# A graph layer's front: small TensorE products beside the edge products, W's parts moved to GpSimd, and row statistics split in two halves

## The reference, cut to what matters

```python
h = jnp.maximum(_layernorm(x, axis=-1), 0.0)
# first layer: attention over the edges
h = h @ W + b_w
s_dst, s_src = h @ a[:512], h @ a[512:]
e = leaky_relu(s_dst[dst] + s_src[src] + b_a, 0.2)
w = exp(e)
out = segment_sum((w / segment_sum(w, dst)[dst])[:, None] * h[src], dst)
x = x + out
# second layer: the same normalisation, 4 experts of two neighbour-mean
# convolutions each, the best two by a gate mixed
```

## Time and profile before

| | us |
|---|---|
| median of 3 runs | 744.05 (743.88 to 745.36) |
| the profiled execution | 744.08 |
| its span in the trace | 742.3 |
| PE busy | 717.8 (97%) |
| DVE busy | 428.0 (58%) |
| ACT busy | 398.1 (54%) |
| POOL busy | 184.1 (25%) |

### The profile page before, as it was taken

The page is one execution under the profiler, slowest core; times in us unless marked ns, Lnnn a source line. Parts: engine busy times, 40 slices in busy tenths (PEclk is TensorE's granted clock), DMA queues, the critical chain, the costliest instruction groups (busy, mean ns, idle before and its releaser), DMA issues.

```text
span 742.3 us, 12047 instructions
## 1 busy us (share of the span) xinstructions
PE 717.8 (97%) x3574; PEld 582.2 (78%) x3574; DVE 428.0 (58%) x1056; ACT 398.1 (54%) x897; POOL 184.1 (25%) x204
## 2 busy tenths in 40 slices
PE   5899999999999999999999999999999999999994
PEld 3589977888888888777777777878888888888883
DVE  8899889999752538622722622657444544444341
ACT  6966769677653521511511511347677667767751
POOL 4000000000000100850300010045666555655511
PEclk9999999999999999999999999999999999999998
DMA  9100000111501247799699695379844994438950
GB/s 207 39 4 3 4 3 18 53 35 35 165 8 58 79 123 240 217 333 326 228 354 328 200 359 197 99 184 264 300 93 88 264 343 120 86 69 225 290 156 6
DMA packets 46444, 115.19 MB, mean 155 GB/s; under 512 B 8340, under 2 KB 8552, under 8 KB 46361
## 3 DMA queue, kind: packets, MB, share of 16 engines
q1 hardware_dynamic: 28581, 77.60, 32.7%
q0 software_dynamic: 9136, 19.65, 11.6%
q10 hardware_dynamic: 8644, 16.86, 6.9%
HBM read 64.89 MB, written 50.08 MB: 155 GB/s over the span
## 4 chain that ended last, share of the span: by engine, by line
PE 92%; DVE 4%; ACT 1%; issue 1%; POOL 0%; DVEq 0%; ACTq 0%; POOLq 0%
PE ps L1783 16%; PE ps L1784 16%; PE ps L1785 16%; PE ps L2185 7%; PE ps L2184 6%; PE ps L2052 3%; PE ps L2053 3%; PE ps L1985 3%; PE ps L1860 3%; PE ps L1979 3%; PE ps L1980 3%; PE ps L2115 2%; PE ps L1923 1%; PE ps L1811 1%; PE ps L1925 1%; PE ps L1924 1%
## 5 line engine op out<-in xcount | busy, mean ns | idle before, releaser
L1110 ACT ACTIVATE agn<-ps,rec 32x128 f32<-32x128 f32 x336 | 120.7, 359 | 38.7 <-PE ps L2185 34.8
L1044 ACT ACTIVATE slots<-he_t 125x512 fp32r<-125x512 f32 x40 | 25.3, 635 | 150.9 <-DVE he_t L1581 146.6
L2185 PE MATMUL ps<-slots,CTs 125*128 x230 | 89.9, 391 | 0.0
L1581 DVE TENSOR_TENSOR he_t<-ps,b_b 125x512 f32<-125x512 f32 x40 | 27.6, 691 | 105.5 <-PE ps L1785 72.3
L728 POOL DMA_INDIRECT hrow<-t_d,piece_i x80 | 76.1, 951 | 25.7 <-issue 23.5
L2184 PE MATMUL ps<-slots,CTs 125*128 x207 | 80.7, 390 | 0.0
L1746 DVE TENSOR_TENSOR tm<-ps,b_b 128x512 f32<-128x512 f32 x23 | 15.9, 692 | 84.3 <-PE ps L1785 84.2
L1783 PE MATMUL ps<-W,agT_hi 128*125 128x512 f32 x160 | 63.5, 397 | 0.0
L1783 PE MATMUL ps<-W,h2T_hi 128*125 128x512 f32 x160 | 63.4, 396 | 0.0
L1785 PE MATMUL ps<-W,agT_lo 128*125 128x512 f32 x160 | 63.3, 396 | 0.0
L1784 PE MATMUL ps<-W,agT_hi 128*125 128x512 f32 x160 | 63.2, 395 | 0.0
(11 more groups left out here) (316 smaller groups left out, 1665.4 us busy)
## 6 DMA issues: line engine op xcount, KB each, us to landing
he_d<-slots SPq DMA_DIRECT2D x30, 448.0 KB
slots<-he_d SPq DMA_DIRECT2D x30, 448.0 KB
w_d<-slots SPq DMA_DIRECT2D x3, 4096.0 KB, 18.7
slots<-w_d SPq DMA_DIRECT2D x24, 512.0 KB
t_d<-he_t SPq DMA_DIRECT2D x40, 224.0 KB
raw<-in_L_gnn_Wl ACTq DMA_DIRECT2D x4, 1024.0 KB, 7.2
raw<-in_L_gnn_Wr ACTq DMA_DIRECT2D x4, 1024.0 KB, 5.6
slots<-in_L_gnn_Wl ACTq DMA_DIRECT2D x4, 1024.0 KB, 10.0
```

The costliest lines, as they stand in the source:

```text
L1110: last = a.activation(agn[32 * r:32 * r + 32, q, :], ps[n, 3 + i % 2, 128 * r:128 * r + 128], ACT.Copy, scale=rec[n, i, 4:5])
L2185: last = mm(o, CTs[:, t, :], part(k, P, t * 1024 + D, P), start=False, stop=t == T - 1)
```

## The change

- **Small products on TensorE.** `wake()` runs 12 products of `ones` and `ident` (128x128, f32) ahead of the first hot block. `keep_busy(bank, n)` runs n products of 250 columns of `onehot_p` whose result is never read: 3 ahead of each hot block from block 11 on, 16 behind the last block, 8 ahead of the first and 4 ahead of each other count step of tile 1. `e_q` and `q_sel` have 128 rows instead of 65; the added rows of `q_sel` are zero.
- **Order of the front.** The small steps of PE stand one or two blocks later. All 22 hot blocks are evicted by ACT. The columns of tile 0 come after block 13 instead of 10, `bias_in(0)` after 17 and `norm(0)` after 18.
- **W's parts by GpSimd.** `W0_hi` (was ACT's) and `W0_lo` (was DVE's) are made by POOL as soon as W is in SBUF, after `a_sum`, the sum of the two vectors a, with which the bias needs one product instead of two.
- **Row statistics in two halves.** Tiles 0 to 4 before tile 0's one-hots, with their own root on ACT and `scales(0)` after the first step of one-hots; tiles 5 to 9 in rounds 1 to 3 of DVE, their root behind `windows_out(3)`, `scales(1)` in round 4.
- **Round 0.** The source vectors are made four before and four after `hT_lo`. PE runs the product with W first, by parts as they come, and then the scores, which wait for `wa` alone; the bias sum is made in round 5 and waited for in the last round.

```diff
@@ -140,18 +140,19 @@
...
         e_g = at("e_g", [CR, CG, P], F32, 12032)
-        e_q = at("e_q", [2 * CR + 1, CG, P], F32R, 15040)
+        e_q = at("e_q", [128, CG, P], F32R, 15040)
...
         q_f = at("q_f", [2 * CR + 1, P], F32, 21408)
-        q_row = at("q_row", [2 * CR + 1, P], F32, 21920)
-        q_at = at("q_at", [2 * CR + 1, CR], F32, 22432)
-        q_sel = at("q_sel", [2 * CR + 1, CR, P], F32R, R1 + 20480)
+        q_row = at("q_row", [128, P], F32, 21920)
+        q_at = at("q_at", [128, CR], F32, 22432)
+        q_sel = at("q_sel", [128, CR, P], F32R, R1 + 20480)
...
         spill = [at(f"spill_{k}", [128, D], F32, R1 + 6144 + 2048 * k) for k in range(2)]
+        a_sum = at("a_sum", [P, D], F32, R1 + 18432)
@@ -618,7 +617,7 @@
...
                                      base=-CR * k, pattern=[[-1, CR]], channel_multiplier=1))
-            link(g.memset(q_at[2 * CR:, :], 1.0))
+            link(g.memset(q_at[2 * CR:2 * CR + 1, :], 1.0))
@@ -646,6 +645,13 @@
...
+            pool.wait_ge(*small_in(48))
+            g.tensor_tensor(a_sum[:], a_b[0:P, 0, :], a_b[0:P, 1, :], ALU.add).then_inc(ab_ready.sem, 1)
+            pool.wait_ge(*w0_in(16))
+            g.tensor_copy(W0_hi[:], W0_f[:]).then_inc(w0_hi_ready.sem, 1)
+            pool.wait_ge(*w0_hi_ready(1))
+            g.tensor_tensor(W0_lo[:], W0_f[:], f32(W0_hi[:]), ALU.subtract).then_inc(w0_lo_ready.sem, 1)
@@ -805,7 +811,13 @@
...
+            def deviations(k):
+                half = slice(k * T // 2, (k + 1) * T // 2)
+                a.activation(std[:, half], std[:, half], ACT.Sqrt).then_inc(std_ready.sem, 1)
...
             def norm(t):
+                if t == T // 2:
+                    act.wait_ge(*norm_ready(2))
@@ -813,12 +825,16 @@
...
                 act.wait_ge(*hw_done(t + 1))
+                if t == 0:
+                    act.wait_ge(*wa_ready(1))
...
                     act.wait_ge(*hw_done(b))
+                if b == 1:
+                    act.wait_ge(*s_done(1))
@@ -836,21 +852,21 @@
...
             for u in range(NU):
-                if u in HOT_ACT:
-                    hot_columns(u)
-                if u == 3:
+                hot_columns(u)
+                if u == 5:
...
                     copy(e_gc[:], ps[0:P, 7, 0:CG * CR]).then_inc(cols_ready.sem, 1)
-                if u == 10:
+                if u == 13:
...
                     act.wait_ge(*var_ready(1))
-                    a.activation(std[:], std[:], ACT.Sqrt).then_inc(std_ready.sem, 1)
-            act.wait_ge(*norm_ready(1))
-            norm(0)
-            act.wait_ge(*w0_in(16))
-            copy(W0_hi[:], W0_f[:]).then_inc(w0_hi_ready.sem, 1)
+                    deviations(0)
+                if u == 17:
+                    bias_in(0)
+                if u == 18:
+                    act.wait_ge(*norm_ready(1))
+                    norm(0)
@@ -865,9 +881,13 @@
...
                     a.activation(spark[:], spark[:], ACT.Exp)
-                bias_in(b)
+                if b > 0:
+                    bias_in(b)
...
                     windows_out(b)
+                if b == 3:
+                    act.wait_ge(*var_ready(2))
+                    deviations(1)
@@ -1151,14 +1171,15 @@
...
             v.memset(q_row[CR:2 * CR, :], -1.0)
+            v.memset(q_row[2 * CR:, :], 0.0)
             link(v.tensor_tensor(q_f[2 * CR:, :], q_f[2 * CR:, :], q_f[2 * CR:, :], ALU.mult))
-            link(v.tensor_scalar(q_row[2 * CR:, :], q_f[2 * CR:, :], -1.0, 1.0, ALU.mult, ALU.add))
+            link(v.tensor_scalar(q_row[2 * CR:2 * CR + 1, :], q_f[2 * CR:, :], -1.0, 1.0, ALU.mult, ALU.add))
...
                 c = slice(8 * k, 8 * k + 8)
-                v.tensor_tensor(q_sel[:, c, :], q_row[:].unsqueeze(1).broadcast_to([2 * CR + 1, 8, P]),
-                                q_at[:, c].unsqueeze(2).broadcast_to([2 * CR + 1, 8, P]), ALU.mult
+                v.tensor_tensor(q_sel[:, c, :], q_row[:].unsqueeze(1).broadcast_to([128, 8, P]),
+                                q_at[:, c].unsqueeze(2).broadcast_to([128, 8, P]), ALU.mult
@@ -1184,20 +1205,15 @@
...
-            def hot_columns(u):
-                dve.wait_ge(*hot_made(u + 1))
-                v.tensor_scalar(onehot_p[:, u * CU:(u + 1) * CU, :].rearrange("p (h c) n -> p h (c n)", h=2),
-                                ps[0:P, u % 3 * 2:u % 3 * 2 + 2, 0:CU // 2 * P], 0.0, None, ALU.max
-                                ).then_inc(hot_dve_ready.sem, 1)
+            def batch_flags(b):
+                more = more_here(dve, b)
+                return more, dve.value_load(tab_b[0:1, b:b + 1, BW + 1:BW + 2], min_val=0, max_val=NW * NG)
...
-            dve.wait_ge(*x_in(32))
-            row_stats(range(0, 2))
-            hot_columns(HOT_DVE[0])
@@ -1216,10 +1232,11 @@
...
             v.tensor_scalar(tab_f[:, 1:2], tab_f[:, 1:2], -1.0, None, ALU.add).then_inc(n_ready.sem, 1)
-            row_stats(range(2, 4))
+            dve.wait_ge(*x_in(32))
+            row_stats(range(0, 1))
...
             v.tensor_copy(tab_f[:, 2:3], ps[0:NW, 7, 0:1]).then_inc(tab_f_ready.sem, 1)
-            row_stats(range(4, T // 2))
+            row_stats(range(1, 2))
@@ -1236,38 +1253,42 @@
...
-            dve.wait_ge(*x_late_in(32))
-            link(row_stats(range(T // 2, T)))
-            for t in range(T):
-                last = v.bn_aggr(x_mv[:, t, :], x_stats[:, t, :])
-            link(last)
-            v.tensor_scalar(std[:], x_mv[:, :, 1], EPS, None, ALU.add).then_inc(var_ready.sem, 1)
+            late = row_stats(range(2, T // 2))
+            dve.wait_ge(*flag_ready(2))
+            dve.wait_ge(*tab_ready(1))
+            first_flags = batch_flags(0)
...
+            def half(k):
+                return slice(k * T // 2, (k + 1) * T // 2)
...
+            def variances(k, last):
+                link(last)
+                for t in range(T)[half(k)]:
+                    last = v.bn_aggr(x_mv[:, t, :], x_stats[:, t, :])
+                link(last)
+                v.tensor_scalar(std[:, half(k)], x_mv[:, half(k), 1], EPS, None, ALU.add).then_inc(var_ready.sem, 1)
...
+            variances(0, late)
...
-            def scales():
-                dve.wait_ge(*std_ready(1))
-                link(v.reciprocal(rstd[:], std[:]))
-                v.scalar_tensor_tensor(shift[:], x_mv[:, :, 0], -1.0, rstd[:], ALU.mult, ALU.mult
+            def scales(k):
+                dve.wait_ge(*std_ready(k + 1))
+                link(v.reciprocal(rstd[:, half(k)], std[:, half(k)]))
+                v.scalar_tensor_tensor(shift[:, half(k)], x_mv[:, half(k), 0], -1.0, rstd[:, half(k)], ALU.mult, ALU.mult
...
             def sources():
-                dve.wait_ge(*w0_in(16))
-                dve.wait_ge(*small_in(48))
-                source_vectors(0)
                 source_vectors(1)
-                for w in range(2):
-                    dve.wait_ge(*wa_f_ready(2 * KC - 1 + w))
-                    v.scalar_tensor_tensor(spill[w][0:P, :], bw_b[:], 1.0, a_b[0:P, w, :], ALU.mult, ALU.mult,
-                                           accum_out=ab[:, w:w + 1]).then_inc(ab_ready.sem, 1)
...
+            def bias_source():
+                dve.wait_ge(*ab_ready(1))
+                v.scalar_tensor_tensor(a_sum[:], bw_b[:], 1.0, a_sum[:], ALU.mult, ALU.mult,
+                                       accum_out=ab[:, 0:1]).then_inc(ab_ready.sem, 1)
                 dve.wait_ge(*ab_ready(2))
-                v.tensor_scalar(s_add[:], ab[:, 0:1], ab[:, 1:2], ba_c[:], ALU.add, ALU.add).then_inc(wa_ready.sem, 1)
...
-            def first_weights_low():
-                dve.wait_ge(*w0_hi_ready(1))
-                v.tensor_tensor(W0_lo[:], W0_f[:], f32(W0_hi[:]), ALU.subtract).then_inc(w0_lo_ready.sem, 1)
+                v.tensor_scalar(s_add[:], ab[:, 0:1], ba_c[:], None, ALU.add).then_inc(wa_ready.sem, 1)
@@ -1286,8 +1307,7 @@
...
             def tile_and_batch(b):
-                more = more_here(dve, b)
-                before = dve.value_load(tab_b[0:1, b:b + 1, BW + 1:BW + 2], min_val=0, max_val=NW * NG)
+                more, before = batch_flags(b) if b > 0 else first_flags
@@ -1301,20 +1321,35 @@
...
                     last.then_inc(step_ready.sem, 1)
+                    if b == 0 and k == 0:
+                        scales(0)
+                    if b == 4 and k == 2:
+                        scales(1)
...
                     product_low(b - 1)
-                else:
-                    scales()
-                    sources()
+                if b == 0:
+                    dve.wait_ge(*w0_in(16))
+                    dve.wait_ge(*small_in(48))
+                    source_vectors(0)
...
                 if b == 0:
-                    first_weights_low()
+                    sources()
+                if b == 1:
+                    dve.wait_ge(*x_late_in(32))
+                    row_stats(range(5, 7))
+                if b == 2:
+                    row_stats(range(7, 9))
+                if b == 3:
```

(61 more changed lines are left out.)

7 lines of the change are left out of this document (2 added, 5 removed).

## The result

The changed kernel took 746.29 us (median; 745.61 to 747.88) against 744.67 (743.88 to 745.42) for the kernel before, a ratio of 1.0029 with a 95% interval of 1.002 to 1.0037. So it is slower by 1.6 us where 2.1 us of gain were forecast. The kernel before has two groups of executions (four at 743.88 to 744.06, four at 745.29 to 745.42) and 744.67 lies between them; against 744.0, near its profiled execution (744.08) and its later medians, the loss is 2.3 us. The profiled execution of the kernel after took 745.61 us, its fastest, with a span of 743.9.

A forecast was written before the change was run, and what follows sets the result against it. The front before 42.96 us, ending in a chain on DVE alone, was taken as the bound. DVE free for tile 1 at 38.7 gives 40.75 - 38.7 = 2.05 us off 744.1: 742.0 us, range 739.8 to 745.8.

The forecast's parts named there:

- The clock and ACT's pace: Front: PE at 2.4 GHz from about 9 us, ACT's 22 blocks every 0.91 us, last done at 32.4 against 34.9.
- rival B: Front: clock not held between early blocks, ACT starves, its end 34 to 35.5; about 743.8 us; chance 0.23.
- S: Moment when DVE is free for tile 1: 37.2 us if nothing holds it, 38.7 with the collision, 42.8 before.
- The collision: Before tile 1: POOL's 3.7 us subtraction blocks DVE's first one-hots of tile 0, costing 1.65 us at the scales; chance 0.38.
- Tiles 1 to 4: On DVE: 6.15 us a tile plus 4.3 us of added work against some 2.6 of slack; gain 40.75 - S.
- The bias sum (1.0) in tile 5: DVE's later rounds: the 1.0 us bias sum and the last tile's wait for it fall into slack.
- PE's limit: Tiles 0 and 1 on PE: 6.8 us, then 6.8 plus 2.6 of small products; at most 4.1 us gained.
- (A): No collision: POOL finds gaps or one-hots don't take its port; gain 3.55, 740.5 us, at best 740.0; chance 0.27.
- (C): Slower: clock stays at 1.2 GHz into blocks with added products, each 1.5 us; 746.5 us; chance 0.12.
- (D): Small products run but move nothing, hidden by DVE's waits; up to 1 us less gain; no chance of its own.

The follow-up runs named there:

- e9: Changed kernel with flags read ahead, statistics undivided, W's low part in four pieces, and no small products (128 rows kept): 741.66 us, ratio 0.9974 to the kernel before.
- e6: Changed kernel with flags read ahead, row statistics undivided and POOL's subtraction for W's low part in four instructions of 512: 741.34 us, ratio 0.9961 to the kernel before.
- e1: Changed kernel with the next round's flags (register loads) read right behind this round's one-hots: 743.37 us, ratio 0.9990 to the kernel before.
- e10: Changed kernel with flags read ahead, statistics undivided and W loaded ahead of x's second half: 743.83 us, ratio 0.9997 to the kernel before.
- e4: Changed kernel without any small product, 128 rows kept: 746.82 us (745.7 to 751.52), ratio 1.0049 to the kernel before.
- e7: e6 without the 24 small products in tile 1: 740.81 us (739.97 to 742.36), ratio 0.9956 to the kernel before.
- e11: Kernel before with only the 128 rows and all the small products added: 747.0 us, ratio 1.0034 to the kernel before.
- e8: Kernel before with only W's high and low parts moved to POOL: 743.12 us, ratio 0.9997 to the kernel before.

## Why the prediction was wrong, step by step

*The clock and ACT's pace: right in its result.* ACT's first hot block starts at 9.80 (forecast 9.75), the last is done at 32.3 (32.4), tile 0 turns at 32.36. The clock did fall at 14 us (rival B's condition), but B's price was not due: ACT waited 0.54 us once. That this was the small products' work is not borne out: e9, without them, is only 1.4 us later at tile 0 (33.62, against 32.21 in e6 and 35.93 before), and how the other 2.3 divide between the 128 rows and the order no run shows.

*S, the moment when DVE is free for tile 1: right without the loads.* Forecast 38.7 with the collision; `wa` ended at 38.06, and the one-hots started at 39.70. The 1.64 us between are the step that failed, here for the first of three times: "DVE is free for tile 1" was taken as the moment when its last instruction ends, and the register loads behind it were put at nothing.

*The collision: mechanism right, victim and size off.* I took 3.7 us for the subtraction, falling on the one-hots. It took 4.55, beyond my bound of two copies (3.78), and fell on `std`, for 4.0 us. The scales were done at 28.28 instead of the 27.15 of my sum without a collision, a delay of 1.1 us instead of 1.65, since W landed earlier (the copy started at 20.45, forecast 21.7). The Trainium skill says of this ("SBUF — State Buffer", who interferes with whom) that the engine that starts first holds the shared ports for its whole instruction; the 4.17, 4.54 and 3.60 us of after, e1 and e10 agree, now for POOL first, and so do e6's four pieces, between which `std` slipped. The Trainium skill's 2.5 cycles an element ("GPSIMD Engine Reference", instruction dispatch) gave an estimate of 4.3; the row shows 4.55, and my own bound was further off.

*Tiles 1 to 4: the same step, the second time.* I wrote that a tile costs DVE 6.15 and the additions 4.3, and that the gain is 40.75 - S. With S = 39.70 that formula gives tile 5 at 72.25. It came at 73.39: 0.98 more on DVE (low part of tile 4 ready at 69.58, not 68.60), the gap of 1.53 behind `std` less 0.55, since a tile and the additions cost DVE a little less than I had put (tile 1 took 7.26 with two statistics of 0.6), and 0.16 on PE. I had counted instructions and left out the sequencer. The warning stood in the profile: 1.33 us of "issue" ahead of the first one-hots of the kernel before, directly behind `std`; 28.23 in the earlier trace rows is where it ends.

*"The bias sum (1.0) in tile 5 ... find DVE with slack again": the same step, the third time.* The bias sum would have; the 1.48 behind it did not. Tile 7 begins 7.76 us behind tile 6 instead of 6.79: 0.97 lost.

*The balance.* Forecast gain 2.05, measured -1.21 at the last tiles: 3.26 apart. Later S 1.0 (1.64 of loads, less 0.64 for the better front), tiles 1 to 4 0.98 + 0.16, tile 6 0.97, and 0.14 since I took 73.3 for a tile 5 that began at 73.16: 3.25.

*PE's limit: right in kind.* With the loads and halves undone, PE bounds: e6's tile 1 takes 49.80 - 40.43 = 9.37 us, forecast 6.8 + 2.6. (The 2.6 are not won by leaving the small products out, since DVE's one-hots then bound the tile.) The limit is 3.0 rather than 4.1 us, because tile 0 took 8.2 instead of 6.8. In the kernel after, its 25 count products take 3.71 us (32.85 to 36.56) without a gap and at a granted clock of 1.00, where I had put 2.9; their lengths alone (0.30 us each) don't say why.

*The rivals.* (A) did not occur: POOL found no gap. (B) occurred in its condition and not in its price. (C), slower by a low clock, had the right sign and nearly the right number (746.5) by luck: no blocks with added products stand 1.5 us apart in the profile after. (D), that the small products move nothing, was the truest of them: e9's median shows 0.3 us. The mechanism that decided was in none.

*What stays open.* The pace of tile 0's count products; what DVE's sequencer does in the 0.55 us behind a step that it has waited for; how the earlier tile 0 divides between the order of the front and the 128 rows, and what the new order of round 0 alone is worth, since none of these was run apart; the wide ranges of e4, e7 and e9; the 0.4 us behind the last tile.

## What to carry to other kernels

Count the sequencer's own work as well as the instructions: wherever a program loads registers or branches right behind a step that it has just waited for, the loads are idle time; put them behind a long queued step (2.3 to 2.9 us in one kernel, 1.1 in the other). Work may be moved "into slack" only as far as that slack goes (0.65 us a tile here), while the place that it left may have been hidden by a wait. An engine's idle time is not free if its instruction holds up a neighbour: cut the long instruction into pieces, so that the neighbour's steps can come between (0.17 to 1.31 us for `std`, which took 2.91 beside one instruction). And price added products by what bounds the tile they stand in: beside DVE's one-hots they cost little here, in a tile that PE bounds their full 2.4 us (e11).

## What the runs showed of the hardware that I had not expected

- Two register loads on DVE behind a wait: gaps of 1.33 to 1.64 us, of which about 0.95 goes if the loads are issued earlier.
- A DVE step of 5 or 10 elements a row took 4.17, 2.91 and 3.60 us beside a subtraction of 2048 elements on POOL, 0.15 to 0.17 otherwise; the statistics (`BATCH_NORM_STATS2`) were not slowed by it (e8: 3.05 us for five).
- POOL's subtraction of 128x2048 took 4.55 us, its copy of the same size 1.89: 2.4 times as long, for twice the operands.
- Tile 0's count products stood 0.142 us apart at a granted clock of 1.00 (3.71 us for 25); those of later tiles 0.108 (2.71).
- The granted clock fell to 0.50 for some 3 us at 14 us while PE was busy without a gap, with 128-row products in it, and rose again; the profiled run of the same kernel with the flags moved (e1) did not show it.
- Edge products of 128 rows ran at the high level from 13.57 us on without any small product (0.72 us a pair in e9); those of 65 rows in the kernel before did not (1.19).
